# Two-layer graph network on one core: the second node stage issued beside the buckets of the first layer, and a shorter table of spilled pieces

## The reference

```
h1 = relu(x[row] @ nbW + nbb);  h2 = relu(x[col] @ selfW + selfb)
log_alpha = concat(h1, h2) @ attW + attb
gate = sigmoid(log(u) - log1p(-u) + log_alpha)
mask = clip(gate * (ZETA - GAMMA) + GAMMA, 0, 1)
d = clip((segment_sum(mask, row) + 1e-6) ** -0.5, 0, 10)
out = segment_sum((mask * d[row] * d[col])[:, None] * x[col], row)
```

## Time and profile before

| | |
|---|---|
| median of three runs | 5892.25 us |
| the profiled execution, its own time | 5890.85 us |
| its span | 5889.1 us |
| PE busy | 4101.6 us, 70% |
| DVE busy | 5129.1 us, 87% |
| ACT busy | 2500.9 us, 42% |
| POOL busy | 1164.4 us, 20% |
| granted TensorE clock, mean | 0.684 of 2.4 GHz |

### The profile page before, as it was taken

How to read it: one execution, slowest core, us unless ns; L and a number is a source line. 1 busy time by engine, 2 the same in 40 slices (tenths; PEclk the granted TensorE clock), 3 DMA queues, 4 the chain that set the end, 5 groups by cost and what they waited for, 6 DMA issues and landing times. The chain is left out here.

```text
span 5889.1 us, 162768 instructions
## 1 busy us (share of the span) xinstructions
PE 4101.6 (70%) x56330; PEld 3657.5 (62%) x56330; DVE 5129.1 (87%) x10832; ACT 2500.9 (42%) x5126; POOL 1164.4 (20%) x1562
## 2 busy tenths in 40 slices
PE   2777777777677888854555477888888725554777
PEld 2666666666445888854444477658888624443676
DVE  8999999999644999989999899509999799999888
ACT  2666666566044555524555200135555325554000
POOL 0000000000000333310000277303333200000776
PEclk9777677777555555556777799755555567777999
DMA  3000000000043666748999799517666579997999
GB/s 73 0 0 0 0 0 0 0 0 0 1 22 130 232 231 233 235 139 305 329 331 330 291 379 378 199 53 233 230 233 230 164 253 330 330 330 281 381 381 348
DMA packets 428687, 1120.74 MB, mean 190 GB/s; under 512 B 206962, under 2 KB 212707, under 8 KB 428023
## 3 DMA queue, kind: packets, MB, share of 16 engines
q1 hardware_dynamic: 316700, 549.97, 29.8%
q0 software_dynamic: 65856, 316.89, 14.2%
q10 hardware_dynamic: 46036, 252.74, 11.3%
HBM read 873.65 MB, written 279.36 MB: 196 GB/s over the span
## 5 line engine op out<-in xcount | busy, mean ns | idle before, releaser
L1611 PE MATMUL psG<-y_window,area 128*128 128x64 bf16 x14976 | 668.2, 217 | 780.4 <-DVE area L1256 665.3
L1611 PEld LDWEIGHTS psG<-y_window,area 128*128 128x128 bf16 x14976 | 624.7, 114 | 824.2 <-issue 504.0
L642 ACT ACTIVATE work<-iota,work 128x149 bf16<-128x149 f32 x2496 | 789.0, 406 | 0.0
L1430 PE MATMUL psG<-area,work 128*128 128x112 bf16 x2496 | 551.1, 390 | 335.4 <-DVE area L978 335.4
L586 POOL DMA_INDIRECT work<-msg_d,widx x396 | 428.3, 1082 | 1655.7 <-issue 1610.4
L1430 PEld LDWEIGHTS psG<-area,work 128*128 128x128 bf16 x2496 | 357.7, 149 | 483.7 <-issue 338.0
L1423 PE MATMUL psG<-work,merge 128*128 128x148 bf16 x4992 | 546.2, 294 | 68.9 <-ACT work L642 68.9
L1624 PE MATMUL psG<-work,edge 128*128 128x192 bf16 x4752 | 447.7, 251 | 202.8 <-DVE edge L1291 202.8
L1423 PEld LDWEIGHTS psG<-work,merge 128*128 128x128 bf16 x4992 | 529.6, 132 | 91.4 <-issue 65.6
L816 ACT ACTIVATE work<-merge 128x1024 bf16<-128x1024 f32 x312 | 330.1, 1058 | 549.4 <-DVE merge L1266 549.4
L1624 PEld LDWEIGHTS psG<-work,edge 128*128 128x128 bf16 x4752 | 412.2, 145 | 238.0 <-DVE edge L1291 163.4
(11 more groups left out here) (268 smaller groups left out, 8280.4 us busy)
## 6 DMA issues: line engine op xcount, KB each, us to landing
msg_d<-work ACTq DMA_DIRECT2D x312, 776.0 KB, 4.5
area<-rlo_d SPq DMA_DIRECT2D x312, 512.0 KB, 4.1
merge<-crel_d SPq DMA_DIRECT2D x312, 512.0 KB, 5.0
area<-crelp_d SPq DMA_DIRECT2D x312, 512.0 KB, 5.6
y_window<-y_d SPq DMA_DIRECT2D x312, 48.0 KB, 3.5
y_d<-cur SPq DMA_DIRECT2D x7, 1008.0 KB, 3.8
y_d<-work SPq DMA_DIRECT2D x7, 1008.0 KB, 4.8
work<-msg_d,widx POOLq DMA_INDIRECT x396, 6.9
```

The source lines that it names most:

```text
L642: ins = act.activation(below[:, h, k, :], iota_all[:, :], ACT.Sign, bias=keyf[:, bass.ds(t * CT + k, 1)], scale=-1.0)
L1430: ins = pe.matmul(psG[:, 2 + h, 0:RECS * CT], place[:, h, :, k], spread_rec[:, h, :, :, k], start=k == 0, stop=k == CT - 1)
L1611: ins = pe.matmul(psG[:, 2 * h + k // CH, k % CH * D:(k % CH + 1) * D], col_one_hots[:, h, k * P:(k + 1) * P], y_window[:, h, m * D:(m + 1 ...
```

## The change

It has two parts, and nothing else is edited.

First, in the first layer the node stage of the second layer is issued inside the bucket stage. DVE now counts each bucket that it has written (`bucket_kept`), in both layers; the output stores of ACT wait for 147 more. ACT gets 49 times `node_beside(g)`, each of the same four copies as before, with buffers of their own and `psR` in place of `psG`. PE gets the same in three steps, one behind the matmuls of each bucket: behind bucket 3g+3 the three transposes of group g, behind 3g+4 the product with the weights, behind 3g+5 the scores. The last group's steps follow the loop. With the local path taken (as it is here), ACT and PE skip the old node stage of the second layer.

Second, the one-hots of 64 and of 8 slots stand side by side in one tile of 72 columns for each bucket, so two matmuls for each bucket do what four did; DVE makes the 8 columns piece by piece (four instructions a piece, in place of two a piece and two ahead). PE's three `turn_column` stand ahead of the spilled pieces.

```diff
@@ vector: one-hots of the spilled pieces
-            for h, (first, lanes) in enumerate(tiles):
-                dve.tensor_tensor(fourth_hots[h][0:lanes, :, :], iota[0:lanes, 0:FOURTH - THIRD]...,
-                                  spill_slot[h][:, HI:2 * HI]..., ALU.is_equal)
             for p_ in range(PIECES):
                 if p_ >= 2:
                     dve.wait_ge(spill_piece_moved, p_ - 1)
                 for h, (first, lanes) in enumerate(tiles):
-                    dve.tensor_tensor(spill_hots[p_ % 2][h][0:lanes, :, :], iota[0:lanes, 0:THIRD]..., ALU.is_equal).then_inc(spill_hots_ready, 1)
+                    for k, (a, z) in enumerate(((0, THIRD), (THIRD, FOURTH))):
+                        ins = dve.tensor_tensor(spill_hots[p_ % 2][h][0:lanes, :, a:z], ..., ALU.is_equal)
+                    ins.then_inc(spill_hots_ready, 1)
@@ tensor
+            pe.wait_ge(records_kept, T)
+            for c, column in enumerate((temps[0], rowf, temps[1])):
+                turn_column(c, column)
             pe.wait_ge(spills_ready, 2)
...
-                        pe.matmul(psR[0:THIRD, 0, 3 * c:3 * c + 3], spill_hots[p_ % 2][h][0:lanes, b, :], row_parts[h][:, c, :], ...)
-                    for h in range(2):
-                        lanes = (P, TAIL)[h]
-                        ins = pe.matmul(psR[THIRD:FOURTH, 0, 3 * c:3 * c + 3], fourth_hots[h][0:lanes, c, :], row_parts[h][:, c, :], ...)
+                        ins = pe.matmul(psR[0:FOURTH, 0, 3 * c:3 * c + 3], spill_hots[p_ % 2][h][0:lanes, b, :], row_parts[h][:, c, :], ...)
                 ins.then_inc(spill_piece_moved, 1)
-            pe.wait_ge(records_kept, T)
-            for c, column in enumerate((temps[0], rowf, temps[1])):
-                turn_column(c, column)
@@ vector, bucket_out
-                    if L == 1:
-                        ins.then_inc(bucket_kept, 1)
-                    elif isinstance(b, int) and b == HI - 1:
-                        ins.then_inc(x_piece_ready, PIECES)
+                    ins.then_inc(bucket_kept, 1)
@@ scalar
+                def node_beside(g):
+                    n = NG + g
+                    act.wait_ge(bucket_kept, (g + 1) * GH)
+                    wait(act, group_transposed, n)
+                    act.activation(x_beside, cur[:, bass.ds(g * (GH * D), GH * D)], ACT.Copy).then_inc(group_staged, 1)
+                    act.wait_ge(group_transposed, n + 1)
+                    wait(act, hidden_multiplied, n)
+                    act.activation(hT_beside, psR[0:D, 0, 0:GH * P], ACT.Copy).then_inc(hT_ready, 1)
+                    act.wait_ge(hidden_multiplied, n + 1)
+                    wait(act, scores_ready, n)
+                    act.activation(rT_beside, psR[:, 1, 0:GH * P], ACT.Relu, bias=bias[1][:, 0:1]).then_inc(rT_ready, 1)
+                    act.wait_ge(scores_ready, n + 1)
+                    act.activation(ab[:, bass.ds(g * GH, GH), :]..., psR[:, 1, GH * P:GH * P + 2 * GH], ACT.Copy).then_inc(scores_kept, 1)
@@ tensor, behind each bucket's 24 matmuls
+                        if L == 0 and (slot_ >= GH or not isinstance(i, int) or i > 0):
+                            node_beside(i * (SLOTS // GH) - 1 + slot_ // GH, slot_ % GH)
+                def node_beside(g, step):
+                    n = NG + g
+                    if step == 0:
+                        wait(pe, hT_ready, n)
+                        pe.wait_ge(group_staged, n + 1)
+                        pe.nop(nofuse=True)
+                        for b in range(GH):
+                            ins = pe.transpose(psR[0:D, 0, b * P:(b + 1) * P], x_beside[:, b * D:(b + 1) * D], ident[:, :])
+                        ins.then_inc(group_transposed, 1)
+                    elif step == 1:
+                        pe.wait_ge(hT_ready, n + 1)
+                        wait(pe, rT_ready, n)
+                        pe.matmul(psR[:, 1, 0:GH * P], W[1][:, :], hT_beside, start=True, stop=True).then_inc(hidden_multiplied, 1)
+                    else:
+                        pe.wait_ge(rT_ready, n + 1)
+                        wait(pe, scores_kept, n)
+                        for b in range(GH):
+                            ins = pe.matmul(psR[:, 1, GH * P + 2 * b:GH * P + 2 * b + 2], rT_beside[:, b * P:(b + 1) * P], att[1][:, :], start=True, stop=True)
+                        ins.then_inc(scores_ready, 1)
```

More of the change, by code:

```diff
@@ L238, in build @@
         iota_rows = y_edge[:, :, :, :].rearrange("p h k d -> p (h k d)").bitcast(i16)[:, 0:P * WIN].rearrange("p (n s) -> p n s", s=WIN)
+        beside = edge[:, 9 * NC + 4 * HR_:15 * NC].bitcast(f32)
+        x_beside, hT_beside, rT_beside = beside[:, 0:GH * D], beside[0:D, GH * D:GH * D + GH * P], beside[:, GH * D + GH * P:GH * D + 2 * GH * P]
         X = [work, cur]
@@ L738, in node_piece, with node_stage @@
                             keep_ab(p_, u - 1)
[L739 to L744, removed]
+                def node_stage():
+                    act.wait_ge(x_piece_ready, L * PIECES + 1)
+                    stage(0, 0)
+                    stage(0, 1)
+                    transposed(0, 0)
+                    steps(act, 0, PIECES, node_piece)
+                    keep_ab(PIECES - 1, GP - 1)
+                if L == 0:
+                    node_stage()
+                else:
+                    with act.If(is_local):
+                        act.nop()
+                    with act.Else():
+                        node_stage()
+                def node_beside(g):
[10 more added lines that the diff above has]
+                    act.wait_ge(scores_ready, n + 1)
+                    act.activation(ab[:, bass.ds(g * GH, GH), :].rearrange("p h t -> p (h t)"), psR[:, 1, GH * P:GH * P + 2 * GH], ACT.Copy).then_inc(scores_kept, 1)
                 def odd_hot(p_, v):
@@ L833, in _ @@
                     store_messages(T - 1, 3)
+                    if L == 0:
+                        steps(act, 0, NG, node_beside)
                 with act.Else():
@@ L846, in _ @@
                 with act.If(is_local):
-                    act.wait_ge(bucket_kept, (p_ + 1) * PH)
+                    act.wait_ge(bucket_kept, HI + (p_ + 1) * PH)
                 with act.Else():
@@ L1512, in node_piece, with node_stage @@
                             scores(p_, u - 1)
-                if L == 1:
+                def node_stage():
+                    transposes(0, 0)
+                    steps(pe, 0, PIECES, node_piece)
+                    scores(PIECES - 1, GP - 1)
+                if L == 0:
+                    node_stage()
+                else:
                     with pe.If(is_local):
@@ L1516, in _ @@
                     with pe.Else():
-                        pe.nop()
-                transposes(0, 0)
-                steps(pe, 0, PIECES, node_piece)
-                scores(PIECES - 1, GP - 1)
+                        node_stage()
                 pe.wait_ge(parts_ready, L + 1)
@@ L1640, in _ @@
                     steps(pe, 0, HI // SLOTS + 1, sum_buckets)
+                    if L == 0:
+                        for step in range(3):
+                            node_beside(NG - 1, step)
                 with pe.Else():
```

14 lines of the change are left out of this document (5 added, 9 removed).

## The result

The changed kernel takes 5667.1 us (median of four runs, 5665.45 to 5668.84) against 5892.76 (5885.24 to 5893.36) for the kernel before: a ratio of 0.962, 95% interval 0.9603 to 0.9637. The forecast was 5669. The profiled execution took 5668.84 us, with a span of 5667.1 against 5889.1.

What follows compares the result with a forecast made beforehand. It took PE to bound the second node stage, four engines closely the buckets, and PE then ACT the spilled pieces. 5890.85 - 173.2 + 6 - 55.0 = 5668.7, said as 5669 us; range 5646 to 5700.

Steps and rivals of the forecast that it cites:

- Part one, removed: Second layer's node stage: moving it beside the buckets takes 177.55 us of DVE's wait for PE off the path.
- The tail: After the last bucket's write: the last group's remaining steps put 4.3 us back on the path.
- The growth of the stage: First layer's bucket stage: added work lengthens it by 0.04 us a bucket, 6 us in all.
- 2 to 5% to spare: Bucket stage: three buckets and a group need 8.21 us of PE, against 8.37 at DVE's best pace and 8.60 mean.
- The order of events: Bucket stage: transposes start about E + 1.3 (E: end of DVE's one-hots); PE at worst 0.2 us late, DVE's slack 1.6.
- Part two: Spilled pieces and column turns: merged products and earlier turns make `logit` start at 1596.7, saving 55.0 us.
- The line through 8 and 64 columns: Spilled pieces: the two old product times, extended to 72 columns, give 0.149 us a product, saving 25.8 us.
- 72 columns as cheap as 128: Rival, spilled pieces: 72-column products cost as little as fast 128-column ones, 20 us more saved, 5649; chance 0.05.
- PE as the bound: Rival, bucket stage: PE sets the pace, stage grows by 25 to 34 us instead of 6, 5688 to 5697; chance 0.17.
- The clock: Rival, bucket stage: PE's clock falls to the lower level, 382 us more, 6045 in all; chance 0.05.
- The merged product without gain: Rival, spilled pieces: merged products are not cheaper, 25.8 us less saved, 5695; chance 0.05.
- ACT late: Rival, before `logit`: early turns don't free ACT in time, up to 27 us back, 5696; chance 0.06 with other losses.

Runs made afterwards that it cites:

- e1: The changed kernel with the old spilled pieces and the old place of the column turning, so the node stage beside the buckets alone: 5725.31 us, ratio 0.9718.
- e4: The changed kernel with the column turns behind the spilled pieces as before, the products still merged: 5696.89 us, ratio 0.9666.
- e5: The changed kernel with 128 weight columns in place of 72 in the spilled products: 5658.15 us, ratio 0.960.
- e3: The changed kernel with four spilled products a bucket as before (64 and 8 slots apart), turns still early: 5697.63 us, ratio 0.9671.
- e9: The changed kernel with 128 weight columns and each piece's 128-lane products before its 28-lane ones, a bank each, added by DVE: 5647.93 us, ratio 0.9586.
- e10: The changed kernel, 72 columns kept, with each piece's 128-lane products before its 28-lane ones, a bank each, added by DVE: 5647.25 us, ratio 0.9585.
- e12: The changed kernel with a bucket's two spilled products in a bank each, added by DVE at the end, lanes still alternating: 5665.96 us, ratio 0.962.
- e2: The kernel before with only the merged spilled products and early column turns, node stage in its old place: 5835.24 us, ratio 0.9902.
- e6: The changed kernel with each group's product with the weights made twice: 5672.49 us, ratio 0.9626.
- e7: The changed kernel with each group's product with the weights made three times: 5702.76 us, ratio 0.968.
- e8: The changed kernel with all three PE steps of a group behind one bucket instead of three: 5789.81 us, ratio 0.9825.
- e11: The changed kernel with three PE steps behind one bucket in three, each of a different group with its input ready: 5670.26 us, ratio 0.9625.

## Why the prediction was right

**Part one, removed.** 177.55 us on the path, all of it PE's: right. With the tail and the growth of the stage 171.3 us are saved (177.55 - 5.22 - 1.0; in the table 226.05 - 54.7), where 167.2 were forecast, and e1 has the part alone at 168.0, give or take 9.

**The tail.** 5.22 us for the forecast 4.3. The step that fell short is the scores, which I put at 0.65 us at the higher clock "which the stage had". In the tail PE waits for ACT's copies with nothing else to do, the window's clock is 0.72, and the scores took 1.44 us, their length at the lower level. Their 0.8 us more is nearly all of the difference. The clock doesn't fall in every tail: in the traces of e1, e4 and e5 it stood at 1.00, the scores took 0.83 us, and the tail, with the same instructions, was 4.5 us. So 4.3 is nearly right for a tail at the higher level, and which level the changed kernel's tail would get, no row on hand could tell.

**The growth of the stage.** +1.0 us for the forecast +6. This is the term that was mis-sized. The allowance of 0.04 us a bucket for register work, late sums and thinner slack came from nothing measured, and nothing of it shows: DVE waits once for a sum of PE's in the whole stage, 1.04 us, at its end, and the stages of the seven other kernels with the same node work in them (e1, e3, e4, e5, e9, e10, e12) take 422.2 to 424.1 us, where e2's, without it, takes 423.0 and that of the kernel before 421.8. The growth can't be told from nothing. PE's need was over-stated as well, 8.21 against 7.9 (e6): the 24 matmuls were put at 2.13 and take 2.03 to 2.10, and the group was put at 1.82 and takes 1.68. The forecast's "2 to 5% to spare" was 6 to 8%. That the changed kernel's own trace shows 8.21 as well is chance. The order of events was right: the transposes start at E + 1.5 (3507.80, with E = 3506.32) for the forecast E + 1.3, and no bucket's sum is late but the last.

**Part two.** -54.9 for -55.0. The line through 8 and 64 columns gave 0.149 us for 72, measured 0.148; the first product came at 1549.17 (1548.8), `logit` at 1596.76 (1596.7), the second logarithm ended at 1541.4 (1540). One number was right for a reason I had wrong: I read the step between 64 and 128 columns (0.14 to 0.03) as one of the weights' width, and most of it was the changing of lanes, 0.08. The rival "72 columns as cheap as 128" (5649) was thus within reach without touching the columns: e10 has 5647.

**The rivals.** PE as the bound: not at this load; it comes with one product of 384 columns more (e6, e7). The clock: 0.99 in the stage. e8 has it fall in half of the groups, by two waits in place a group of 1.25 us together; the changed kernel has one of 0.5 us in every second group (24 in the stage, 11.6 us). e6 and e7, which add f32 work and no waits, leave it at 1.00. The merged product without gain, and ACT late: neither (e4, e3).

**What the sum hid.** The forecast of the time, 2 us off, is better than its terms: part one was 4.1 us better than said, and 4.1 us were lost in layer 1, which the forecast left at its old length. Its three stages, from the windows of either kernel, are 737.2, 745.2 and 450.8 us before and 738.9, 746.2 and 451.4 after, with 0.8 more ahead of them: about 0.2% everywhere, at the same busy times and clocks. The other traces settle whose these are. From the split to the end the kernel before takes 1947.4 us and the changed one 1951.5, and the other twelve, whose layer 1 is the same code behind the split, lie between 1946.7 (e11) and 1951.6 (e5), with 1947.1 in e6 and 1951.1 in e8. e6, e7 and e11 have both parts of the change and stand within 0.7 us of the kernel before. So the 4.1 us are the scatter of single executions, not the change. That they made up for the 4.1 us by which part one beat its forecast was luck.

## What to carry to other kernels

A stage can be laid under the one ahead of it for next to nothing if its engines have that much room there (PE was busy for 331 of 422 us, ACT for none) and each step is put where its input is ready long before, on an in-order engine above all: e8 and e11 do the same work at the same place in the program and differ by 120 us through waits in place and the clock that fell behind them. Set the engine's need against the covering stage's mean pace, and measure that need by doubling one instruction until no gap is left (e6): rows that hold gaps overstate it. And where small products alternate between two tile heights, do one height after the other first and count columns afterwards.

## What the hardware showed that I had not expected

- Small products that alternate between 128 and 28 lanes of rows cost 0.08 us each over the same products in order, at a clock of 0.50 in all of them (e9, e10 against e5, e12), more than the whole product of 128 columns (0.033 us). That makes e10 the fastest kernel here, 5647.25 us, 0.9585 of the time before (0.9569 to 0.9601) and about 20 us below the changed one.
- The granted clock fell to 0.53 for 3.6 us behind 3.5 us in which PE was busy for 2.25 (e8), and was at 1.00 in the next window. Behind the next group, with the same waits, it stayed at 1.00. The same work without the waits in place kept 0.99 (e11).
- 24 matmuls of 192 columns and some 3 us of f32 work a group beside them (e7; 9.29 less three times 2.1) held 1.00, while f32 work of the same kinds by itself had 0.51, with PE busy for 176.56 us of 178.
